# A GELU evaluated twice: ScalarE writes the rounded high part itself, VectorE's copy is dropped

## What is computed

```python
ln_out = layernorm(hidden_states, ln1_s, ln1_b)
q, k, v = jnp.split(ln_out @ w_qkv + b_qkv, 3, axis=-1)
x = hidden_states + attention(q, k, v, ltor_mask) @ w_ao + b_ao          # A
q = layernorm(x, ln2_s, ln2_b) @ w_q + b_q
k, v = jnp.split(encoder_states @ w_kv + b_kv, 2, axis=-1)
x = x + attention(q, k, v, cross_mask) @ w_co + b_co                     # B
ln_out = layernorm(x, ln3_s, ln3_b)
x = x + gelu(ln_out @ w1 + b1) @ w2 + b2                                 # M
a = _layer_norm(audio_kv, ln_gamma, ln_beta)
return x + tanh(gate) * (attention(x @ Wq.T, a @ Wk.T, a @ Wv.T) @ Wo.T) # C
```

## Time and profile before

| | |
|---|---|
| time, median of 3 runs | 963.01 us (961.67 to 965.79) |
| the profiled execution's own time | 968.34 us |
| its span | 966.5 us |
| granted TensorE clock, mean | 0.956 |
| TensorE busy | 884.2 us, 91% |
| VectorE busy | 696.9 us, 72% |
| ScalarE busy | 576.2 us, 60% |
| GpSimd busy | 560.1 us, 58% |

### The profile page before, as it was taken

The page is one execution under the profiler, slowest core; times in us unless marked ns, Lnnn a source line. Parts: engine busy times, 40 slices in busy tenths (PEclk is TensorE's granted clock), DMA queues, the critical chain, the costliest instruction groups (busy, mean ns, idle before and its releaser), DMA issues.

```text
span 966.5 us, 24365 instructions
## 1 busy us (share of the span) xinstructions
PE 884.2 (91%) x9808; PEld 827.5 (86%) x9808; DVE 696.9 (72%) x1463; ACT 576.2 (60%) x1073; POOL 560.1 (58%) x565
## 2 busy tenths in 40 slices
PE   5678789999999999999999999999999999998885
PEld 5577788999999898989999998989999998987774
DVE  4366767779697877878697877878787877775533
ACT  4235555758484766658584856657584847665342
POOL 1327383939476574929475675929385765836221
PEclk9657999999999999999999999999999999998996
DMA  6021000010101010010101010010101010000000
GB/s 213 1 67 40 23 19 12 2 52 1 41 13 41 13 30 24 2 52 2 41 12 42 12 41 13 1 53 1 52 1 42 13 41 2 24 19 1 24 12 12
DMA packets 33005, 26.74 MB, mean 28 GB/s; under 512 B 12672, under 2 KB 32000, under 8 KB 32896
## 3 DMA queue, kind: packets, MB, share of 16 engines
q1 hardware_dynamic: 32896, 25.20, 8.9%
HBM read 20.99 MB, written 4.19 MB: 26 GB/s over the span
## 4 chain that ended last, share of the span: by engine, by line
PE 51%; DVE 31%; issue 6%; POOL 6%; ACT 4%; DMA 1%; SPq 0%; DVEq 0%; ACTq 0%; POOLq 0%
PE pj L418 15%; PE pj L436 10%; PE s_bank L499 8%; PE s_bank L485 6%; DVE prob_AC L893 5%; PE s_bank L474 4%; PE pj L449 4%; DVE vz_AC L885 3%; DVE h_hi L1097 3%; DVE rmax_B L898 3%; DVE stats L933 2%; DVE x L917 2%; DVE oT_AC_lo L863 2%; POOL h_lo L1139 2%; DVE vz_B L885 2%
## 5 line engine op out<-in xcount | busy, mean ns | idle before, releaser
L1112 POOL TENSOR_TENSOR rstd<-var_eps,half 128x2 f32<-128x2 f32 x64 | 47.5, 743 | 233.3 <-DVE var_eps L944 233.3
L1132 POOL TENSOR_TENSOR prob_AC<-prob_AC,rmax_C 128x512 f32<-128x512 f32 x64 | 66.2, 1046 | 111.6 <-DVE rmax_C L898 109.2
L707 ACT ACTIVATE k<-pj,kbias,consts 128x256 f32<-128x256 f32 x192 | 93.0, 572 | 51.1 <-PE pj L418 51.1
L474 PE MATMUL s_bank<-k,q 64*128 64x128 f32 x1536 | 107.4, 284 | 7.6 <-ACT q L694 3.9
L474 PEld LDWEIGHTS s_bank<-k,q 64*128 64x128 f32 x1536 | 92.4, 188 | 19.7 <-ACT q L691 6.4
L1139 POOL TENSOR_TENSOR h_lo<-g,h_hi 128x512 fp32r<-128x512 f32 x64 | 83.7, 1328 | 9.8 <-DVE h_hi L1097 9.8
L1126 POOL TENSOR_TENSOR prob_B<-prob_B,maskB_off 128x512 f32<-128x512 f32 x64 | 81.3, 1304 | 11.3 <-DVE prob_B L893 11.3
L1126 POOL TENSOR_TENSOR prob_AC<-prob_AC,maskA_off 128x512 f32<-128x512 f32 x64 | 80.7, 1285 | 5.2 <-DVE prob_AC L893 5.2
L485 PE MATMUL s_bank<-consts,prob_AC 128*128 128x128 f32 x512 | 71.7, 285 | 12.3 <-POOL prob_AC L1132 12.3
L449 PE MATMUL pj<-w_hi_M,h_hi 128*128 128x256 f32 x256 | 77.8, 304 | 5.0 <-issue 3.3
L715 ACT ACTIVATE prob_AC<-s_bank 128x512 f32<-128x512 f32 x128 | 68.1, 596 | 17.6 <-PE s_bank L485 17.4
(11 more groups left out here) (195 smaller groups left out, 3001.1 us busy)
## 6 DMA issues: line engine op xcount, KB each, us to landing
x_in<-in_x SPq DMA_DIRECT2D x16, 256.0 KB, 2.7
ctx_b<-in_ctx_features SPq DMA_DIRECT2D x16, 256.0 KB, 3.0
ctx_c<-in_ctx SPq DMA_DIRECT2D x16, 256.0 KB, 3.3
out<-y SPq DMA_DIRECT2D x16, 256.0 KB, 2.2
g<-in_w_M SPq DMA_DIRECT2D x2, 1024.0 KB, 6.8
maskB<-in_mask_Bx1xSxS_ff SPq DMA_DIRECT2D x32, 64.0 KB, 2.7
prob_AC<-in_w_A_qkv SPq DMA_DIRECT2D x1, 768.0 KB, 4.5
prob_B<-in_w_B_kv SPq DMA_DIRECT2D x1, 512.0 KB, 6.2
```

Source lines behind the costliest of these rows:

```text
L474: mm = nc.tensor.matmul(bank[:, c, :, b2, :], q2[rows_, c, t * TILE + b2].rearrange("p e q -> p (e q)"), k2[rows_, c, t * TILE + b2], star ...
L707: last = nc.scalar.activation(k2[:, m, :, s, :], k_all[:, m], ACT.Identity, bias=kbias[:, "ABC".index(a), s, m:m + 1], scale=parity[:, 2 + ...
L1132: nc.gpsimd.tensor_tensor(p3, p3, rmax[a][:, r, :].unsqueeze(2).broadcast_to([P, BL * TILE, S]), ALU.subtract).then_inc(shifted[a], 1)
```

## The change

ScalarE evaluates the GELU of each tile twice from the same PSUM bank, with the same bias: first into `g` (f32), then into `h_hi` (rounded to f32r), and frees the bank after the second. `high_h` and its four calls in VectorE's body are gone. The wait that `high_h` had for M.Y1 of the iteration before, the last reader of the old `h_hi`, moves to ScalarE, ahead of the second pair of evaluations. `low_h` on GpSimd waits for the bank's free count, which ScalarE raises, in place of VectorE's `h_hi_done`.

```diff
@@ sem
-        gelued, h_hi_done, h_lo_done = sem("gelued"), sem("h_hi_done"), sem("h_lo_done")
+        gelued, h_lo_done = sem("gelued"), sem("h_lo_done")
@@ gelus(m, i), ScalarE
                 for k in range(2):
                     c = BH + 2 * m + k
-                    last = nc.scalar.activation(g[:, m, k, :], bank[:, k * TOK:(k + 1) * TOK],
+                    nc.scalar.activation(g[:, m, k, :], bank[:, k * TOK:(k + 1) * TOK],
+                                         ACT.Gelu_apprx_tanh, bias=bias[:, c:c + 1])
+                if not isinstance(i, int) or u:
+                    act.wait_ge(pj_full[pj_bank("M.Y1")], pj_use("M.Y1", i - 1))
+                for k in range(2):
+                    c = BH + 2 * m + k
+                    last = nc.scalar.activation(h_hi[:, 2 * m + k, :], bank[:, k * TOK:(k + 1) * TOK],
                                                 ACT.Gelu_apprx_tanh, bias=bias[:, c:c + 1])
                 last.then_inc(pj_free[pj_bank(name)], 1)
@@ body(i), VectorE (four calls, with their "if active")
-                    high_h(0, i)
-                    high_h(1, i)
...
-                    high_h(2, i)
...
-                    high_h(3, i)
@@ VectorE
-            def high_h(m, i):
-
-                u = unit("M", i)
-                if not isinstance(i, int) or u:
-                    dve.wait_ge(pj_full[pj_bank("M.Y1")], pj_use("M.Y1", i - 1))
-                dve.wait_ge(pj_free[pj_bank(f"M.H{m}")], pj_use(f"M.H{m}", i))
-                nc.vector.tensor_copy(h_hi[:, 2 * m:2 * m + 2, :], g[:, m, :, :]).then_inc(h_hi_done, 1)
@@ low_h(m, i), GpSimd
-                pool.wait_ge(h_hi_done, GELU * u + m + 1)
+                pool.wait_ge(pj_free[pj_bank(f"M.H{m}")], pj_use(f"M.H{m}", i))
```

More of the change, by code:

```diff
@@ L1009, in body @@
                     moments("A", x_in, unit("P", i))
-                if active("M", i):
-                    high_h(0, i)
-                    high_h(1, i)
                 if active("B", i):
```

## The result

The changed kernel took 982.46 us (median of 4, 980.99 to 985.5) beside 964.10 us for the kernel before (median of 4: the three runs known before and one of 965.19); the ratio is 1.0195, with a 95% interval of 1.0165 to 1.0224. It is slower, by 18.4 us. The profiled execution took 980.99 us, its span 979.2.

What follows compares the result with a forecast made beforehand. TensorE was taken as the bound, busy 52.35 of 53.80 us a period. Loop 16.3 plus ends 2.9 - 0.4 gave 18.8, say 19 us, on a median of 963.0: 982 us, range (8 in 10) 964 to 1002.

Steps and rivals of the forecast that it cites:

- the mechanism named: ScalarE reaches oT_AC_hi 1.46 us late; VectorE's order passes this to A's masked scores, for which TensorE waits.
- VectorE idle 5.23 us before oT_AC_lo: Sign in the profile after: VectorE idle some 4 to 5 us before oT_AC_lo, its largest new wait.
- a wait of 1.60 us at L485: Sign in the profile after: TensorE waits 1.5 to 1.8 us for A's masked scores at L485.
- ScalarE adds 0.365 us an evaluation, no table load: ScalarE's GELUs: eight more evaluations a period at 0.365 us each, 2.92 us in all, without added table loads.
- The two waits absorb 0.74 and 0.72 us: ScalarE's waits before the third GELU tile and oT_AC_hi take up 0.74 and 0.72 us, leaving 1.46 us lateness.
- 0.21 us of it is swallowed at B's last transposes; net 1.25 us a period: TensorE's 0.21 us wait for the fourth masked scores disappears, so 1.46 us lateness costs 1.25 us a period.
- the loop's term: Iterations 4 to 16, 13 of them, at 1.25 us each: 16.3 us.
- VectorE's relief is worth at most 0.33 us a period by itself: Dropping VectorE's copies closes only TensorE's hole at C's transpose: at most 0.33 us a period, if ScalarE is in time.
- The rival that VectorE was the bound: Removing the copies closes TensorE's holes of 0.33, 0.33 and 0.21 us: 0.87 us a period, 952 us; chance 0.10.
- The ends add 2.5 us: Outside the loop: 2.9 us more in the last GELU iteration, 0.4 us less in the first.
- A fall of TensorE's clock in the new hole: Rival: the longer hole before B's second transpose lowers TensorE's clock, 1.5 us a period, up to 1002 us; chance 0.18.
- The shared port: VectorE's copies and GpSimd hold a shared port pair against each other; GpSimd's gain was put at nothing.

Runs made afterwards that it cites:

- e4: The changed kernel with A's masked scores and value copy moved ahead of C's low part in VectorE's order; 957.17 us, ratio 0.9905.
- e7: The changed kernel with the second pair of evaluations of tile 3 moved behind oT_AC_hi on ScalarE; 970.81 us, ratio 1.0059.
- e1: The changed kernel without the first evaluation (g never written): VectorE's relief without ScalarE's added cost; 955.12 us, ratio 0.9888.
- e2: The kernel before with a second evaluation added for every tile, VectorE still copying: cost without relief; 982.64 us, ratio 1.0170.
- e6: The changed kernel with only tiles 0, 1 and 3 evaluated twice and tile 2 copied by VectorE; 969.70 us, ratio 1.0045.
- e5: The kernel before with A's masked scores and value copy moved ahead of C's low part in VectorE's order; 962.86 us, ratio 0.9986.
- e9: e1 with e4's order on VectorE, so e4 without the second evaluation; 953.90 us, ratio 0.9887.
- The second leaves 2.2 us: The second measurement: the changed kernel timed once more without an edit; 980.95 us, ratio 1.0162, 16.4 us over the kernel before.

## Why the prediction was right, and where its steps were off

The time was forecast at 982 us and came out at 982.46, by the mechanism named: e4 and e7 show the place, e1 and e2 the two parts. The signs in the profile came as well: VectorE idle 5.23 us before oT_AC_lo (4 to 5 forecast), a wait of 1.60 us at L485 (1.5 to 1.8), a period of 54.87 us (55.05). Point by point:

*ScalarE adds 0.365 us an evaluation, no table load.* Right: e6 and the changed kernel differ by 0.74 us a period for two evaluations, and ScalarE's instructions rose from 1073 to 1201, by the 128 evaluations and nothing else. The Trainium skill's figures (ScalarE: Activation LUTs, What ACT_TABLE_LOAD costs) gave 400 ns and 986 us in place of 982, both too high here; its rule that every function costs the same agrees with the trace, where a pair of GELUs and the pair of oT_AC_hi, which is no GELU, both take 0.84 us.

*The two waits absorb 0.74 and 0.72 us.* Mis-sized. They absorbed more: 2.92 us of added work made oT_AC_hi 1.22 us late, not 1.46. A wait had also broken the overlap of neighbouring evaluations (a pair takes 0.84 us by itself and 0.73 behind another); with the wait filled, the overlap comes back, 0.11 us at each.

*0.21 us of it is swallowed at B's last transposes; net 1.25 us a period.* The first is right (no hole at 572.39). The net was 1.22 - 0.21 = 1.01, as the eleven like intervals have it, or 1.06 over all twelve; the loop's term is then 13 x 1.06 = 13.8 us in place of 16.3, 2.5 too much by the lateness that was mis-sized.

*VectorE's relief is worth at most 0.33 us a period by itself.* Too low: 0.50 (e1). I had overlooked that the 0.21 us hole hung on the same copies, through GpSimd's queue (e5). It made no difference to the sum, because behind ScalarE's lateness the relief is worth nothing (e2 has the period of the changed kernel). The rival that VectorE was the bound was thus right in part about the kernel before (0.50 us a period, where it had 0.87) and wrong about the changed one.

*The ends add 2.5 us.* Not settled. In the last iteration with a GELU the profile shows the lateness:

```profile
933.36 3.63 PE L499 MATMUL s_bank<-vz_AC,prob_AC 128*64 128x34 f32 x64 [3.48 <-issue]
...
941.26 0.36 PE L449 MATMUL pj<-w_hi_M,h_hi 128*128 128x256 f32 x1 [0.87 <-ACT h_hi L742]
```

C's value products wait 3.48 us where they waited 1.06. The windows view, with the columns as above, first the kernel before, then the changed one; in each the first window goes from iteration 16's oT_AC_hi to B's last output projection, the second from there to M.Y0:

```profile
828.83:898.18 69.35, 61.04 (x704) 57.29 (x705) 46.37 (x95) 35.84 (x65) 36.54 (x35) 0.95 0.05 15
898.18:928.62 30.44, 25.15 (x237) 23.43 (x237) 13.59 (x35) 15.55 (x28) 11.13 (x12) 0.89 0.07 19
```

```profile
840.60:907.00 66.40, 58.24 (x680) 54.53 (x677) 41.39 (x90) 38.42 (x74) 33.61 (x33) 0.97 0.06 16
907.00:941.26 34.26, 26.08 (x236) 24.34 (x237) 12.54 (x31) 18.44 (x36) 10.88 (x13) 0.85 0.05 17
```

The second window is 3.8 us longer. TensorE's idle time in it rose from 5.29 to 8.18 us, by the 2.9 forecast; the rest is busy time at a lower mean clock, 0.85 beside 0.89. But the first window, which I had put at nothing, is 2.95 us shorter. Its idle time is nearly the same, 8.31 and 8.16 us: TensorE no longer waits 1.78 us for C's output, but waits 2.70 us for C's value products where it waited 1.22. The other 2.80 us are busy time. The mean clock was higher, 0.97 beside 0.95, and 24 matmuls fewer fall in the window; which part is whose wasn't tried. In these two profiles what lies outside the twelve intervals comes to nothing (spans 12.7 us apart, intervals 12.8). In the medians 2.2 to 4.6 us are left beside the 13 periods, with intervals of some 3 us either way, and e4 beside e9 has 2.8.

*A fall of TensorE's clock in the new hole.* It did not come: the clock was 1.00 over the 6 us around a hole of 1.36 us, and 1.00 over all of the steady loop, from 182.14 to 840.60. It agrees with the hole of 1.52 us in the earlier trace rows that had no fall behind it.

*The shared port.* The Trainium skill (SBUF — State Buffer, Who interferes with whom) has GpSimd held up by such copies too, which I left at nothing. The trace agrees with it: h_lo went from 1328 to 1277 ns in the mean, and e5 beside e4 has GpSimd slower by 0.2 us at each of two places. In the changed kernel it makes no difference, since e2, with the copies, has the same period; once A's masked scores no longer stand behind oT_AC_hi, these operations are on e5's chain, and what they lose is part of the 0.67 us between e5 and e4.

That the sum met the first median to 0.5 us is luck: it had 2.5 us too much in the loop, and this measurement leaves 4.6 us outside it where 2.5 were forecast. The second leaves 2.2 us, so that against its 16.4 us the 18.8 of the forecast are 2.4 too much, which is the loop's error. The mechanism was right; the size of the lateness was not.

## What to carry to other kernels

Adding work to an engine that is idle a third of the time costs nothing only as far as it fits into the waits between its start and the next instruction that another engine queues behind; count those waits (here 0.74 and 0.72 us, and 0.1 us each for the overlap they broke), and take the rest at full price. Two works that end at one meeting point don't add but compete: measure the relief and the cost each alone, for the larger hides the smaller. And before an edit is thrown away, look at what stands in order behind the late instruction without needing it: moving two masked scores ahead of a low part turned a loss of 1.06 us a period into a gain of 0.73, which neither edit had by itself.

## What was not expected of the hardware

An evaluation of 128x256 back to back costs 0.365 us while its own duration in the trace grows: 475 ns in the mean before, 494 and 507 in the changed kernel (L736, L742), up to 622. Durations of neighbours that overlap are no prices; the distance of their starts is.

The start-up of one kernel varies by several us from execution to execution: oT_AC_hi of A in iteration 2, ahead of the first GELU, began between 95.20 and 98.19 us in twelve profiles of kernels that are the same up to there. Differences of the spans of two profiles (12.7 us here, where the medians differ by 18.4 and 16.4) say less than their steady periods.
